# Written-out attention loop, an early first gather, and a gate pass in two column groups

## The reference

```python
q, k = ctx @ Wq.T + bq, ctx @ Wk.T + bk            # ctx (4, 1024, 512), q and k 128 wide
x = x + layernorm(x) @ softmax(q @ k.T).T           # per batch, x (4, 1024, 1024)
h = layernorm(x)
top4, idx = top_k(h @ gate_w.T + gate_b, 4); w = softmax(top4)      # 32 experts
gate = min(h @ w_gate[e] + b_gate[e], 7)            # 1024 -> 512
up   = clip(h @ w_up[e] + b_up[e], -7, 7)           # 1024 -> 512
y   += w * (((up + 1) * gate * sigmoid(1.702 * gate)) @ w_down[e] + b_down[e])   # 512 -> 1024
out  = x + y
```

## Time and profile before

| what | us |
|---|---|
| median of three runs (3228.62 to 3232.39) | 3232.22 |
| time of the profiled execution | 3231.47 |
| its span, first to last instruction | 3229.7 |
| PE busy | 3088.9 |
| DVE busy | 1719.9 |
| ACT busy | 1294.6 |
| POOL busy | 594.1 |

### The profile page before, as it was taken

The page is one execution under the profiler, slowest core; times in us unless marked ns, Lnnn a source line. Parts: engine busy times, 40 slices in busy tenths (PEclk is TensorE's granted clock), DMA queues, the critical chain, the costliest instruction groups (busy, mean ns, idle before and its releaser), DMA issues.

```text
span 3229.7 us, 46840 instructions
## 1 busy us (share of the span) xinstructions
PE 3088.9 (96%) x15456; PEld 1612.5 (50%) x15457; DVE 1719.9 (53%) x2851; ACT 1294.6 (40%) x1299; POOL 594.1 (18%) x502
## 2 busy tenths in 40 slices
PE   6799899995999999999999999999999999999997
PEld 3465555553444554545545455454554455544553
DVE  3577777774453544554544545554455445554432
ACT  3453444422342433443443434443343434443421
POOL 0023333332111111111111111111111111111111
PEclk8899999997999999999999999999999999999998
DMA  4133323253564555656555657565566555565433
GB/s 152 65 113 124 106 99 107 95 187 125 155 170 110 156 150 156 196 165 192 150 156 151 184 153 206 163 192 142 151 180 173 172 156 150 155 173 133 117 59 59
DMA packets 210439, 468.03 MB, mean 145 GB/s; under 512 B 57761, under 2 KB 57761, under 8 KB 210114
## 3 DMA queue, kind: packets, MB, share of 16 engines
q0 software_dynamic: 45856, 152.33, 21.4%
q10 hardware_dynamic: 94576, 225.46, 20.9%
q1 hardware_dynamic: 69938, 89.38, 8.5%
HBM read 354.64 MB, written 112.46 MB: 145 GB/s over the span
## 4 chain that ended last, share of the span: by engine, by line
PE 75%; DMA 1%; issue 0%; ACT 0%; DVE 0%; SPq 0%; POOL 0%; POOLq 0%
PE psG L1245 23%; PE psU L1245 23%; PE psY L1267 23%; PE psX L1251 4%; PE psA L1258 2%; DMA acc<-y,idxs 0%; DMA idxs<-slots 0%; DMA xg<-xn_tab,idxg 0%; DMA idxg<-slots 0%; DVE y L1192 0%; ACT y L1126 0%; ACT xT L1115 0%; SPq L1041 0%; POOL acc L1083 0%; SPq L1042 0%
## 5 line engine op out<-in xcount | busy, mean ns | idle before, releaser
L1245 PE MATMUL psG<-W,xT 128*128 128x512 f16 x3456 | 771.7, 380 | 2.9 <-ACT xT L1115 2.9
L1267 PE MATMUL psY<-W,aT 128*128 128x512 f16 x3456 | 769.4, 379 | 1.5 <-ACT aT L1119 1.5
L1245 PE MATMUL psU<-W,xT 128*128 128x512 f16 x3456 | 769.4, 379 | 0.0
L1245 PEld LDWEIGHTS psG<-W,xT 128*128 128x128 f16 x3456 | 338.5, 98 | 412.6 <-issue 5.2
L1267 PEld LDWEIGHTS psY<-W,aT 128*128 128x128 f16 x3456 | 338.1, 98 | 377.2 <-ACT aT L1119 1.7
L1245 PEld LDWEIGHTS psU<-W,xT 128*128 128x128 f16 x3456 | 338.2, 98 | 375.6
L123 DVE SCALAR_TENSOR_TENSOR W<-stage,W 128x2048 f16<-128x2048 f32 x192 | 438.7, 2285 | 3.8 <-ACT W L118 3.8
L1192 DVE SCALAR_TENSOR_TENSOR y<-bias,idxs,y 128x1024 f32<-128x1024 f32 x144 | 185.0, 1285 | 460.3 <-ACT y L1126 460.3
L1083 POOL DMA_INDIRECT acc<-y,idxs x144 | 226.3, 1571 | 990.4 <-DVE y L1192 974.9
L118 ACT ACTIVATE W<-stage 128x2048 f16<-128x2048 f32 x192 | 365.8, 1905 | 48.5 <-issue 37.9
L650 PE MATMUL psM<-W,XT 128*128 (+1 forms) x1392 | 369.9, 384 | 10.8 <-issue 9.1
(11 more groups left out here) (140 smaller groups left out, 2372.5 us busy)
## 6 DMA issues: line engine op xcount, KB each, us to landing
stage<-in_L_ffn_w_down ACTq DMA_DIRECT2D x62, 1024.0 KB, 6.6
stage<-in_L_ffn_w_up ACTq DMA_DIRECT2D x61, 1024.0 KB, 7.2
stage<-in_L_ffn_w_gate ACTq DMA_DIRECT2D x60, 1024.0 KB, 8.3
stage<-in_x SPq DMA_DIRECT2D x32, 512.0 KB, 4.8
xr<-in_x SPq DMA_DIRECT2D x32, 512.0 KB, 4.4
acc<-xr SPq DMA_DIRECT2D x32, 512.0 KB, 3.1
xn_tab<-x2h SPq DMA_DIRECT2D x32, 512.0 KB, 3.0
bias<-in_L_ffn_b_down ACTq DMA_DIRECT2D x32, 512.0 KB
```

The costliest lines, as they stand in the source:

```text
L1245: op = pe.matmul(ps[:], xT[:, k, :, a], weights(par, c, offset + k * I, I), start=k == 0 and n == 0, stop=k == KH - 1 and n == 2)
L1267: op = pe.matmul(psY[:, h * HALF:(h + 1) * HALF], aT[:, k, :, a], weights(par, c, 2 * KH * I + k * H + h * HALF, HALF), start=k == 0 and n ...
```

## The change

1. `schedule` writes the three iterations out in Python (`for b in range(B - 1)`), with `more` a Python boolean; `guarded` takes True and False, so that no run-time branch is left there.
2. Steps 0 and 1 also use `both` (where batch b2 has a step behind it and `more` is not False). The last probability tile's transposes move from step 0 into `queries_and_keys`, before its second quarter. In `both`, the transposes of xs2 stand before matmuls 10 to 17 in place of 6 to 13, the logits before 2 to 9 of the second half in place of 0 to 7.
3. The first tile's index load and gather are issued at the end of stage one, on SP and POOL, before the block's end; the buffers `idxg` and `xg` become common to both stages.
4. The last tile gets buffers of its own (`idxs_last`, `y_last`), its index load waits for nothing, and its scatter alone waits for the one before.
5. The gate pass of an expert's first tile is issued as two column groups of 64 rows of the tile: 48 matmuls of 64 stationary columns by 512, with 48 weight loads, in place of 24 and 24.

```diff
 def guarded(eng, cond, body):
-    if cond is None:
+    if cond is None or cond is True:
         body()
-    else:
+    elif cond is not False:
...
-            with eng.Fori(0, B - 1) as b:
+            for b in range(B - 1):
                 more = b < B - 2
...
+            for t in range(2):
+                sp.wait_ge(s_slotout[t], 16 * TOPK * (B * NT // 2))
+            sp.dma_start(g["idxg"][:], slots[0:P, :]).then_inc(g["s_idxg"], 16)
...
-            for t in range(2):
-                pool.wait_ge(s_slotout[t], 16 * TOPK * (B * NT // 2))
+            pool.wait_ge(g["s_idxg"], 16)
+            pool.indirect_dma_start(out=g["xg"][:], out_offset=None, in_=xn_tab[:, :],
+                                    in_offset=bass.IndirectOffsetOnAxis(g["idxg"][:, 0:1].bitcast(U32), 0)).then_inc(g["s_xg"], 16)
...
                 for n in range(4):
+                    if n == 1 and not first(bk):
+                        pe.wait_ge(s_xTev, NT * batch(bk))
+                        pe.wait_ge(s_alo, NT * batch(bk))
+                        transpose_words(ah_w[(NT - 1) % 2], s_AT)
...
+                held = range(10, 10 + KH)
                 def x2_beside(m):
-                    if m == 6:
-                        alone(pe, s_xTev, tile(b1, s), s_past)
+                    if m == held[0]:
+                        if s == 0:
+                            pe.wait_ge(s_ATev, tile(b2, NT))
+                        else:
+                            pe.wait_ge(s_xTev, tile(b1, s))
                         pe.wait_ge(s_xs2, tile(bt, n + 1))
...
             tt = start_of(sp, E)
-            alone(sp, s_added, tt, s_past)
-            load_slots(sp, idxs, tt - 1, s_idxs)
+            load_slots(sp, idxs_last, tt - 1, s_idxl)
...
-            def rows_times(ps, par, offset, done):
+            def rows_times(ps, par, offset, done, groups=1):
+                rows = P // groups
                 for k in range(KH):
                     for n, (a, c) in enumerate(PASSES):
-                        op = pe.matmul(ps[:], xT[:, k, :, a], weights(par, c, offset + k * I, I),
-                                       start=k == 0 and n == 0, stop=k == KH - 1 and n == 2)
+                        for r in range(groups):
+                            op = pe.matmul(ps[r * rows:(r + 1) * rows, :], xT[:, k, r * rows:(r + 1) * rows, a],
+                                           weights(par, c, offset + k * I, I),
+                                           start=k == 0 and n == 0, stop=k == KH - 1 and n == 2)
...
-                rows_times(psG, par, 0, s_G)
+                rows_times(psG, par, 0, s_G, groups=2 if first else 1)
```

## The result

The changed kernel takes 3206.82 us (median of four runs, 3203.51 to 3207.2), the kernel before, measured beside it, 3230.80: ratio 0.9924, 95% interval 0.9907 to 0.9941. The profiled execution has a span of 3205.4 us. The range held; the time is 12 us under the 3219 forecast.

The account below looks back on a forecast made before the run. PE's own time bounds stage two; in stage one DVE bounds short steps, PE long ones. 3231.5 - 14.3 (stage one) - 4.2 (gather) - 5.2 (last tile) + 10.6 (gate pass) = 3218.4, plus 0.75 to the median: 3219 us; range 3202 to 3388.

Parts of the forecast that it names:

- The gate pass in two groups: 32 first-tile gate passes in stage two: halves run at once, mode changes cost 0.33 us a pass, 10.6 us; bounds 0, 17.
- The forecast's case: First-tile gate passes: a pair takes one matmul's 0.2158 us, only changes between whole and halved array priced; chance 0.55.
- The serial rival: First-tile gate passes: the two matmuls of a pair stream one after the other, 165.7 us more, 3385; chance 0.22.
- The rival of loads that show: First-tile gate passes: half-width weight loads can't hide, 98 ns more for each pair, 75 us, 3294; chance 0.12.
- The early gather: Between stage one and stage two: PE starts at 769.8 in place of 774.04, gain 4.2 us; bounds 0 and 5.7.
- The last tile: Kernel's end: with its own buffers ACT weighs y from 3209.6 in place of 3214.86, gain 5.2 us; bounds 4.5 and 5.3.
- The loop: Stage one's attention loop written out: two returns go, 13.1 us less 1.5 for DVE, gain 11.6 us.
- Steps 0 and 1 and the place of the transposes: Stage one, woven steps 0 and 1 and transposes at 10: 2.4 + 2.1 - 1.8, gain 2.7 us.
- three steps 1: Stage one: woven, each loses its excess over DVE's 17.86 us, 0.5 to 1.0 each, gain 2.4 us together.
- the two stretches with queries and keys and step 0: Stage one: transposes moved between the quarters cost up to 0.9 us for each of two batches, 1.8 us lost.
- That DVE paces the short steps: Stage one, steps without context: DVE is the bound at 17.86 us, so hiding PE's stalls there gains nothing.
- the rival in which all of PE's stalls count: Stage one gains 24 us as every PE stall pays, and the array switch is free: 3199 us; chance 0.04.

Follow-up runs that it names:

- `groups_only`: The kernel before with only the first tile's gate pass in two column groups; 3240.98 us against 3231.73 before.
- `loop_only`: The kernel before with only the attention loop written out and its branches gone; 3215.98 us, ratio 0.9955.
- `quarters`: The changed kernel with four column groups of 32 rows, 96 matmuls, in the first tile's gate pass; 3205.32 us, ratio 0.9918.
- `whole_gate`: The changed kernel with the first tile's gate pass whole again, 24 matmuls of 128 stationary columns; 3195.68 us, ratio 0.9893.
- `at_six`: The changed kernel with the transposes of xs2 back before matmuls 6 to 13 and the logits before 0 to 7; 3209.60 us, ratio 0.9931.
- `dve_longer`: The changed kernel with two more small DVE operations, each waited for, in late steps that have both batches; 3213.29 us, ratio 0.9941.
- `half_after_half`: The changed kernel with all 24 gate matmuls of the first column group before all 24 of the second; 3344.39 us, ratio 1.0349.
- `threes`: The changed kernel with the first tile's 48 gate matmuls in alternating blocks of three of each half; 3206.59 us, ratio 0.9919.
- `sixes`: The changed kernel with the first tile's 48 gate matmuls in alternating blocks of six of each half; 3221.65 us, ratio 0.9970.

## Why the prediction was right, and where its sizes were off

- **The gate pass in two groups: right.** The forecast's case (halves at once, only the changes priced) is what the trace shows. 0.33 a pass was priced, 0.27 measured; 10.6 us against 9.0 by the two traces and 9.3 by `groups_only`. The serial rival comes near only when the order is half after half (4.30 us a pass of its 5.18). The rival of loads that show is refuted: a half-width load lasts 112 ns on the mean, 14 more than a whole one, and hides; the 32-column loads of `quarters` last 98 and hide with four to a slot. The forecast chose this case from a row on supply alone, since no row showed two matmuls at once; that choice came out.
- **The early gather: right.** 4.2 was expected and 4.4 found, and for the reason given. The trace names PE's own queue at the block's opening (PEq) in place of the gathered rows as what PE waited for the earlier trace rows. The block opens 11.7 us after the issue of the last slot store (734.44 to 746.12), which is what the forecast's terms add up to (757.99 to 769.7).
- **The last tile: right.** ACT began 0.09 us after the last pass's end; 5.2 against 5.4.
- **The loop: right on the returns, too small beside them.** 11.6 was expected and the two steps give 11.5 in `loop_only`, but that kernel gained 15.8. Of the rest, the nine short steps became shorter, by 0.13 on the mean, 1.2 us in all, and the steps with context became 0.06 longer, 0.5 us. Gaps before waits are shorter in the short steps, and what the code has lost there is waits against a register's value and branches; that it is the register waits was not tested alone. Most of what is left is where the clock fell in the two traces, as shown with `loop_only`.
- **Steps 0 and 1 and the place of the transposes: the step that failed in size, and in one term in sign.** The text allowed 2.7 us. Stage one gained 23.5 by the traces, 14.3 forecast, and about 8 of it are beyond the loop (3216.0 for `loop_only` against 3206.8 with the gains of the other parts, 9.8, and the loss of the groups, 9.0, taken out: 3207.6). Between the same adds of the two traces, 23.4 us split as follows:

| term | forecast | measured |
|---|---|---|
| the two steps after a return | 11.6 | 12.1 |
| three steps 1 | 2.4 | 1.8 + 1.1 + 1.2 = 4.1 |
| seven steps with context, transposes at 10 | 2.1 | 2.9 |
| the two stretches with queries and keys and step 0 | -1.8 | +2.5 and -0.9 = +1.6 |
| nine short steps and the last batch's step 0 | 0 | 2.3 |
| start of the first add | 0 | 0.3 |

The fourth row failed most, by 3.4 us. At the first stretch the trace of before had the lower clock (34.81 us against 32.30), at the second the changed kernel had it (33.10 against 33.99). The moved transposes did not cause either: `loop_only`, which doesn't move them, had 1.00 there and took 33.05 and 33.02; `whole_gate`, which moves them, also had 1.00 and took 32.28 twice. At like clock each stretch became 0.8 shorter, not 0.9 longer. DVE's rows show how: the first maximum of step 0, its split of x2h, and the add that ends it, before (second stretch) and after (first), both at 1.00.

```profile
470.81 1.23 DVE L841 TENSOR_REDUCE mx<-psE 128x1 f32<-128x1024 f32 x1 [2.08 <-PE psE L598]
476.50 1.42 DVE L865 SCALAR_TENSOR_TENSOR x2h<-xs,x2h 128x1024 f16<-128x1024 f32 x1 [0.76 <-ACT x2h L551]
485.02 1.23 DVE L918 SCALAR_TENSOR_TENSOR xr<-psM,xr 128x1024 f32<-128x1024 f32 x1
```
```profile
297.77 1.23 DVE L873 TENSOR_REDUCE mx<-psE 128x1 f32<-128x1024 f32 x1 [2.08 <-PE psE L614]
302.57 1.36 DVE L897 SCALAR_TENSOR_TENSOR x2h<-xs,x2h 128x1024 f16<-128x1024 f32 x1
310.67 1.21 DVE L947 SCALAR_TENSOR_TENSOR xr<-psM,xr 128x1024 f32<-128x1024 f32 x1
```

From the add before to that maximum it is 18.89 us before and 19.40 after: the moved transposes do cost 0.5, of the 0.9 priced. From the maximum to the add it is 14.21 and 12.90: step 0 gains 1.3. The forecast called step 0 DVE's, rightly, and gave it nothing; what it overlooked is that DVE waits 0.76 us there for ACT, which in the plain form copies a tile of probabilities before x2h and in the woven form makes x2h first. Step 1 has the same wait of DVE (0.77) before and not after. So the gain of step 1 was forecast from a stall of PE for ACT's x2T, while the step was already DVE's, and 0.77 of its 1.1 here is this wait. No run changed ACT's order alone; it is read from the rows and the code. The short steps were put at nothing as well; of their 2.3, part comes with the written-out code and part is in the two splits of DVE, as said with `loop_only`.

- **That DVE paces the short steps: right,** against the rival in which all of PE's stalls count, though that rival's 24 us for stage one is nearly what stage one gained, for other reasons. `at_six` and `dve_longer` show it from both sides. The stalls of PE for xs2, up to 1.3 us before, are at most 0.6 after, and the steps shrank only from 17.86 to 17.60.

The forecast of 3219 was 12 us too high, and nearly all of it is in stage one.

## What to carry to other kernels

Two column groups of an fp16 product gain nothing when all rows are needed, and cost little: they stream at once as long as each matmul's partner on the other half stands close behind it in the program (with no more than three waiting matmuls passed over), and each turn from whole to divided array and back costs about 0.27 us. In a stage where PE reads 95% busy, look at the interval of one fixed row of each other engine per step and at what it waited for; where that row never waits for PE, time hidden on PE pays nothing. Writing out a loop whose body is long paid here for its returns, 6 us each. And before two traces of one stage are compared, the granted clock of each stretch has to be laid beside them: here it makes up to 4.4 us between executions of equal code.

## What was not expected of the hardware

- Matmuls on one half of the array start ahead of waiting ones on the other half that stand before them in the program: four ran early in `half_after_half`, and `threes` and `sixes` behaved as if three waiting ones, and no more, can be passed over. The Trainium skill (TensorE: Matmul & The Clock Gate, Part 3: Packing small matmuls — row/col tiling) says that matmuls start and end strictly in program order; these runs differ from it.
- PE was supplied with 96 matmuls and 96 weight loads in 5.30 us, 0.055 us for one with its load. The fastest row of before had 0.07.
- A weight load of 64 columns takes 112 ns on the mean, one of 128 and one of 32 take 98; all were hidden in every form tried.
- The granted clock fell after the same 1.9 us wait of PE in some executions and not in others of the same stage-one code (0.95 against 1.00 over the stretch with queries and keys, 0.83 against 1.00 over the step 0 of the last batch).
